# First softmax of a graph layer: its flags made in the gather's stage, its leaky function on ScalarE and TensorE, its loop rows shared out over two stages

## The reference

```
e = jnp.einsum('ehd,hd->eh', src, a_src) + jnp.einsum('ehd,hd->eh', dst, a_dst)
e = e + edge_bias
e = jnp.where(e > 0, e, ALPHA * e)                                  # ALPHA = 0.2
max_per_node = jax.ops.segment_max(e, col, num_segments=num_nodes)
exp_scores = jnp.exp(e - max_per_node[col])
sum_per_node = jax.ops.segment_sum(exp_scores, col, num_segments=num_nodes)
attn = exp_scores / jnp.maximum(sum_per_node[col], 1e-12)
msg = src * edge_gate * attn[..., None]
```

## Time and profile before

| what | value |
|---|---|
| profiled execution, its own time | 8693.18 us |
| its span, first to last instruction | 8691.1 us |
| mean granted TensorE clock (1.0 is 2.4 GHz) | 0.772 |
| busy: TensorE, VectorE, ScalarE, GpSimd | 5916.9, 6071.0, 1746.5, 6425.4 us |
| `stage_gate` | 52.5 to 2115.9 us |
| `stage_softmax` | 2115.9 to 2288.0 us |
| `stage_aggregate` | 2288.0 to 2858.2 us |
| `stage_first_update` | 2858.2 to 2968.5 us |
| `stage_move` | 2968.5 to 5130.6 us |

### The profile page before, as it was taken

One profiled execution on the slowest core, in us unless ns is written; L12 is line 12 of the kernel. 1 busy time (PEld: TensorE's weight loads), 2 busy tenths in 40 slices (PEclk: granted clock), 3 DMA queues, 4 the chain that ended last, 5 costly groups with the idle time before them and its releaser, 6 DMA issues. The chain is left out here.

```text
span 8691.1 us, 192168 instructions
## 1 busy us (share of the span) xinstructions
PE 5916.9 (68%) x40472; PEld 4854.3 (56%) x40473; DVE 6071.0 (70%) x12108; ACT 1746.5 (20%) x5063; POOL 6425.4 (74%) x7809
## 2 busy tenths in 40 slices
PE   6666666665788587777777549999588830566442
PEld 4455555553677466666666437777378720455332
DVE  5555555556777887777777448888599899898335
ACT  1111111111211444444444102222500010111000
POOL 6777777776788377777777778887277778877774
PEclk6555555555899799999999669999799965899555
DMA  6778888875477266666666669998189953798664
GB/s 198 218 216 219 219 217 220 218 219 168 130 210 211 70 212 205 207 206 206 207 206 207 211 196 268 273 270 239 35 245 263 260 145 87 197 255 237 163 163 110
DMA packets 1900193, 1739.84 MB, mean 200 GB/s; under 512 B 163065, under 2 KB 1624495, under 8 KB 1899807
## 3 DMA queue, kind: packets, MB, share of 16 engines
q1 hardware_dynamic: 1216980, 816.75, 32.2%
q10 hardware_dynamic: 496812, 471.17, 19.3%
q0 software_dynamic: 186160, 449.72, 18.5%
HBM read 1285.39 MB, written 452.43 MB: 200 GB/s over the span
## 5 line engine op out<-in xcount | busy, mean ns | idle before, releaser
L1877 POOL DMA_INDIRECT z_xg<-table,srci x1664 | 1781.6, 1071 | 512.7 <-issue 457.4
L1414 POOL DMA_INDIRECT sorted<-e_score,srci x1612 | 1628.2, 1010 | 602.8 <-issue 427.2
L461 POOL DMA_INDIRECT g_xg<-table,srci x1612 | 1553.9, 964 | 539.5 <-issue 470.0
L481 PE MATMUL g_psg<-g_wg,g_eT 128*128 128x136 f32 x3224 | 1027.5, 474 | 0.0
L1957 PE MATMUL z_ps<-z_wrow,z_oh 128*128 128x132 f32 x3712 | 652.1, 330 | 501.9 <-issue 332.6
L1735 PE MATMUL n_ps<-n_row,n_oh 128*128 128x257 f32 x3712 | 881.2, 389 | 93.2 <-DVE n_row L1711 79.3
L1957 PEld LDWEIGHTS z_ps<-z_wrow,z_oh 128*128 128x128 f32 x3712 | 559.4, 228 | 594.6 <-issue 557.3
L481 PEld LDWEIGHTS g_psg<-g_wg,g_eT 128*128 128x128 f32 x3224 | 769.3, 324 | 191.9 <-issue 191.9
L1735 PEld LDWEIGHTS n_ps<-n_row,n_oh 128*128 128x128 f32 x3712 | 677.7, 190 | 298.0 <-issue 216.4
L479 PE MATMUL g_psg<-g_bias,g_ones 3*128 3x272 bf16 x806 | 318.4, 395 | 675.6 <-DVE g_es L570 646.8
L1473 PE MATMUL m_psx<-acc,e_score 128*128 x3608 | 600.5, 317 | 197.8 <-DVE e_score L1598 122.9
(11 more groups left out here) (426 smaller groups left out, 12696.0 us busy)
## 6 DMA issues: line engine op xcount, KB each, us to landing
n_row<-sorted SPq DMA_DIRECT2D x464, 520.0 KB, 4.4
z_buf<-gathered ACTq DMA_DIRECT2D x464, 256.0 KB
g_keys<-dst_row ACTq DMA_DIRECT2D x451, 256.0 KB, 3.8
ag_buf<-gated SPq DMA_DIRECT2D x451, 256.0 KB, 3.3
m_keys<-dst_row ACTq DMA_DIRECT2D x451, 256.0 KB
gathered<-z_xg SPq DMA_DIRECT2D x416, 256.0 KB
gated<-g_y SPq DMA_DIRECT2D x403, 256.0 KB
g_eT<-in_attr_t SPq DMA_DIRECT2D x402, 256.0 KB
```

The lines of the kernel that those rows point to most:

```text
L461: nc.gpsimd.indirect_dma_start(out=xg[:, u, j, :], out_offset=None, in_=v.table[:, :], in_offset=bass.IndirectOffsetOnAxis(ap=v.srci[:, t: ...
L481: last = nc.tensor.matmul(psg[u % 2][:, h, j * W:(j + 1) * W], eT[:, u % R, (h * H + j) * P:(h * H + j + 1) * P], wg[:, :], start=False, s ...
L1414: nc.gpsimd.indirect_dma_start(out=v.sorted[:, :], out_offset=bass.IndirectOffsetOnAxis(ap=place[:, t:t + 1], axis=0), in_=rows[:, u, j, : ...
L1877: nc.gpsimd.indirect_dma_start(out=xg[:, u, j, :], out_offset=None, in_=v.table[:, :], in_offset=bass.IndirectOffsetOnAxis(ap=v.dsti[:, t: ...
```

## The change

It has five parts.

1. The flags are made in `stage_gate`, by the same eight VectorE instructions, in bf16 in place of f32, from a window of destinations that SP loads into the space of `y`. They stand ahead of the stage's first one-hots.
2. The leaky function leaves VectorE. ScalarE makes `bent`, the absolute value of 0.4 times the head's scores, one instruction for each head. `turn_in` then makes 0.6 times the score plus `bent` with two ordinary matmuls a block (against `steep`, which is 0.6 times the identity, and against the identity) in place of one transpose.
3. Loop rows go in groups of four. Five groups (20 rows) stay in `stage_softmax`. The other 29 are scattered at the end of GpSimd's list in `stage_first_update`, with two buffer sets.
4. The four writes to `firsts` are issued by SP with the loads of the groups 4 to 7 of `stage_gate`.
5. `stage_move` takes `lo` and `hi` over from `stage_gate`. GpSimd fills `rows` with ones, ScalarE copies the keys into `facts`, and ScalarE no longer waits for `s_split`.

```diff
@@ stage_gate
+                sp.dma_start(win[:, 0:TR], window).then_inc(s_win, 16)
...
                 def load(g, u, use):
                     if later(g, R):
                         sp.wait_ge(s_gpe, g - R + 1)
+                    if isinstance(g, int) and R <= g < R + 4:
+                        sp.wait_ge(s_none, 1)
+                        sp.dma_start(empty[:, (g - R) * TR:(g - R + 1) * TR], none[:, :]).then_inc(s_empty, 16)
...
-                sp.wait_ge(s_none, 1)
-                for n in range(4):
-                    sp.dma_start(empty[:, n * TR:(n + 1) * TR], none[:, :]).then_inc(s_empty, 16)
...
+                flagged = chain(dve, s_fl)
+                dve.wait_ge(s_win, 48)
+                for d, (r, g) in enumerate(((fl.rf, fl.gf), (fl.rb, fl.gb))):
+                    way = slice(None, None, -1) if d else slice(None)
+                    edge = TR - 1 if d else 0
+                    flagged(nc.vector.tensor_tensor(r[:, :], win[:, 1:TR + 1], win[:, 2 * d:2 * d + TR], ALU.not_equal))
+                    flagged(nc.vector.tensor_scalar(r[:, :], r[:, :], -BIG, None, ALU.mult))
+                    flagged(nc.vector.tensor_tensor_scan(g[:, way], r[:, way], r[:, way], 0.0, ALU.min, ALU.min))
+                    flagged(nc.vector.memset(r[:, edge:edge + 1], -BIG))
+                dve.wait_ge(s_fl, 8)
@@ new, called by stage_softmax (first=0, last=5, one set) and stage_first_update (5 to 13, two sets)
+def loop_rows(nc, v, pool, loops, s_lp, done, s_loop, first, last):
+    sets, LR = len(s_loop), LOOP_ROWS
+    for n, q in enumerate(range(first, last)):
+        at = n % sets
+        if n >= sets:
+            pool.wait_ge(s_loop[at], 16 * LR * (n // sets))
+        some = min(LR, NB - q * LR)
+        nc.gpsimd.tensor_scalar(loops[:, at, 0:some, TAKING + 1], v.blk[:, q * LR:q * LR + some], v.part[:, 0:1], None,
+                                ALU.add).then_inc(s_lp, 1)
+        pool.wait_ge(s_lp, done + n + 1)
+        for i in range(some):
+            b = q * LR + i
+            nc.gpsimd.indirect_dma_start(
+                out=v.sorted[:, :], out_offset=bass.IndirectOffsetOnAxis(ap=v.loop_at[:, b:b + 1], axis=0),
+                in_=loops[:, at, i, :], in_offset=None).then_inc(s_loop[at], 16)
...
@@ stage_softmax
                         for k in range(a, z):
-                            last = nc.tensor.transpose(ps_in[m % 2][:, (k - a) * P:(k - a + 1) * P], e[:, k::KR, h],
-                                                       v.ident[:, :])
+                            to = ps_in[m % 2][:, (k - a) * P:(k - a + 1) * P]
+                            nc.tensor.matmul(to, e[:, k::KR, h], steep[:, :], start=True, stop=False)
+                            last = nc.tensor.matmul(to, bent[:, k::KR], v.ident[:, :], start=False, stop=True)
...
+                def bend(h):
+                    if h:
+                        act.wait_ge(s_tin, h * len(parts))
+                    nc.scalar.activation(bent[:, :], e[:, :, h], ACT.Abs, scale=0.4).then_inc(s_leaky, 1)
+
+                bend(0)
                 take(0)
+                bend(1)
                 for t in range(H + 3):
                     if 0 <= t - 3 < H:
                         give(t - 3)
                     if t + 1 < H:
                         take(t + 1)
+                    if t + 2 < H:
+                        bend(t + 2)
...
-                    if t + 2 < H:
-                        leaky(t + 2)
@@ stage_first_update, GpSimd
+                nc.gpsimd.memset(loops[:, :, :, :], 0.0).then_inc(s_lp, 1)
...
+                loop_rows(nc, v, pool, loops, s_lp, 2, s_loop, LOOPS_FIRST, -(-NB // LOOP_ROWS))
@@ stage_move
+                nc.gpsimd.memset(rows[:, :, :, :], 1.0).then_inc(s_set, 1)
...
-                    else:
-                        act.wait_ge(s_split, 5)
...
+                for n, key in ((2, v.srck), (3, v.dstk)):
+                    nc.scalar.activation(facts[:, :, n], key, ACT.Copy).then_inc(s_facts, 1)
+                act.wait_ge(s_facts, 2)
+                act.wait_ge(s_set, 1)
...
-                nc.vector.memset(rows[:, :, :, :], 1.0).then_inc(s_set, 1)
...
-                link(nc.vector.tensor_scalar(lo_i, v.srci[:, :], P - 1, None, ALU.bitwise_and))
```

More of the change, by code:

```diff
@@ L612, in _, with stage_softmax @@
                 nc.vector.tensor_copy(hist[:, :], psc[:, 0:NBX]).then_inc(s_end, 1)
-def stage_softmax(nc, v, e, hist, run, below):
-    H, SETS, LR = X8, 4, 5
+def loop_rows(nc, v, pool, loops, s_lp, done, s_loop, first, last):
[13 more added lines that the diff above has]
+                in_=loops[:, at, i, :], in_offset=None).then_inc(s_loop[at], 16)
+    for at in range(sets):
+        rows = sum(min(LR, NB - q * LR) for n, q in enumerate(range(first, last)) if n % sets == at)
+        pool.wait_ge(s_loop[at], 16 * rows)
+LOOP_ROWS, LOOPS_FIRST = 4, 5
+def stage_softmax(nc, v, e, hist, run, below, fl):
+    H, SETS = X8, 4
     sem = v.sem
-    s_b, s_bpe, s_win, s_fl, s_whole = (sem("b_" + n) for n in ("dve", "pe", "win", "fl", "whole"))
-    s_lp, s_pad, s_loop = sem("l_lp"), sem("l_pad"), v.pool_dma_sem("l_loop")
+    s_b, s_bpe, s_fl, s_whole = (sem("b_" + n) for n in ("dve", "pe", "fl", "whole"))
+    s_lp, s_pad, s_loop = sem("l_lp"), sem("l_pad"), [v.pool_dma_sem("l_loop")]
     s_neg, s_tin, s_v, s_vb = sem("f_neg"), sem("f_tin"), sem("f_v"), sem("f_vb")
@@ L797, in _ @@
                 flagged = chain(dve, s_fl)
[L798 to L805 removed]
+                nc.vector.tensor_copy(edges[:, 0:1], gf[:, TR - 1:TR])
+                flagged(nc.vector.tensor_copy(edges[:, 1:2], gb[:, 0:1]))
                 nc.vector.memset(carry[:, :, 0, 0:1], -BIG)
@@ L1184, in stage_first_update @@
     s_x, s_tr, s_xt, s_h, s_row = (sem("u_" + n) for n in ("x", "tr", "xt", "h", "row"))
+    s_lp, s_loop = sem("u_lp"), [v.pool_dma_sem(f"u_loop{n}") for n in range(2)]
     with ExitStack() as mem:
@@ L1337, in _, with stage_move @@
                         rows(i - 5)
-def stage_move(nc, v, held, run, steps, follows, below, sorted_steps, spare):
+def stage_move(nc, v, held, run, steps, follows, below, sorted_steps, spare, split):
     sem = v.sem
     R, U, S = 4, 4, SLOTS
-    s_split, s_set, s_fix = sem("m_split"), sem("m_set"), sem("m_fix")
+    s_split, s_set, s_fix, s_facts = sem("m_split"), sem("m_set"), sem("m_fix"), sem("m_facts")
     s_oh, s_cnt, s_run, s_ohtb = (sem("r_" + n) for n in ("oh", "cnt", "run", "ohtb"))
@@ L1544, in _ @@
                 nc.vector.memset(ohhi[:, :, :, 1, :], 0.0).then_inc(s_fix, 1)
-                for n, key in ((2, v.srck), (3, v.dstk)):
-                    nc.vector.tensor_copy(facts[:, :, n], key)
                 def onehots(g, u, use):
@@ L2567, in build @@
             e_score = sb("e_score", [P, TR, X8], F32, layer)
-            stage_gate(nc, v, e_score, gated, hist, steps_e)
-            recycle(nc, v)
-            stage_softmax(nc, v, e_score, hist, run, below)
+            split = [sb("src_" + k, [P, TR], BF16, layer) for k in ("lo", "hi")]
+            with ExitStack() as until:
+                fl = Env()
+                fl.rf, fl.rb, fl.gf, fl.gb = (sb("node_" + k, [P, TR], BF16, until) for k in ("rf", "rb", "gf", "gb"))
+                stage_gate(nc, v, e_score, gated, hist, steps_e, fl, split)
+                recycle(nc, v)
+                stage_softmax(nc, v, e_score, hist, run, below, fl)
             acc = sb("acc0", [P, NBX, W], F32, layer)
@@ L2575, in build @@
             recycle(nc, v)
-            stage_move(nc, v, held, run, steps_e, follows, below, steps_s, flat(e_score[:, :, :]))
+            stage_move(nc, v, held, run, steps_e, follows, below, steps_s, flat(e_score[:, :, :]),
+                       split)
         both.close()
```

86 lines of the change are left out of this document (30 added, 56 removed).

## The result

The changed kernel took 8710.01 us (median of 8 runs, 8703.09 to 8713.82) where the kernel before took 8678.96 (8 runs, 8674.83 to 8685.21): 1.0031 times as long, 95% interval 1.0022 to 1.004. The forecast was 8633 us, faster by 46 us. It became slower by 31 us. The two profiled executions differ by 21 us (spans of 8691.1 and 8712.1 us); the one of before lies 14 us above the median of its runs, the one of after 4 us, and the traces can only explain those 21 us.

The account below looks back on a forecast made before the run. GpSimd was taken to bound gather and move, VectorE the softmax's steady turns, ScalarE the first update. Terms 8 - 7.7 - 36 + 0 - 11 = -46.7 us gave 8633 us, likeliest range 8620 to 8648.

Parts of the forecast that it names:

- The step that failed: Softmax, TensorE: the new `turn_in` priced as 52 passes, 11.2 us cold or 5.6 warm, 7.7 when beginning cold.
- Rival A: Softmax: TensorE's clock stays at 1.2 GHz, softmax about 205 us instead of 172, net +22, 8702 us; chance 0.04.
- A second step: Softmax steady turns: ScalarE adds one `bend` to 5.42 us of its turn and stays far below the bound.
- Gate, head: Gate's start: flags added on VectorE delay GpSimd's gathers; 8 us longer, bounds 0 and 10.
- the row of 4.03 us: Softmax before: a scatter issued beside the flags' scan took 4.03 us, a plain one 0.97; basis for 8 us in the gate.
- Gate, tail: Gate's end: without SP's four late writes the next stage starts earlier; -7.7 us, bounds -5.5 and -8.
- Move: Move's set-up: fill on GpSimd and copies on ScalarE bring the first scatter earlier; -11 us, bounds -14 and -4.
- End of the softmax: Softmax ends with ScalarE's last exponential instead of a DMA; next stage 0.5 us later, at softmax start + 135.5.
- rival B: First update: loop rows, at 3.2 us a row, outlast the update; +21 us, 8654 us; chance 0.10.
- Update: First update: GpSimd's fill and 29 loop rows stay hidden, landing at most to 2946, before ScalarE ends at 2964.3; 0 us.
- The tail of 34.9 us behind `forward(7)`: Softmax: from `forward(7)` to the last exponential's end, without leaky or `turn_in`, so 34.9 us was to stay.
- Rival C: Softmax: VectorE binds, not TensorE, 11.9 us a turn, and `turn_in(0)` warm; about -9 more, 8624 us; chance 0.05.

## Why the prediction was wrong

**The step that failed** is in the softmax, "A `turn_in` of 26 matmuls is 52 passes like those of `turn_out`: 0.215 us a pass at a clock of 0.50 and 0.107 at 0.98". All 52 passes were priced by contiguous loads. The passes aren't alike. `turn_out` takes its stationary operand from 128 neighbouring elements; `turn_in` takes it with steps of 416 bytes (`e[:, k::KR, h]`) and 52 bytes (`bent[:, k::KR]`). Removing one step took that matmul from 0.51 to 0.22 us with nothing else changed on TensorE; removing the other took it from 0.64 to 0.22, where only the other operand changed too, from `steep` to the identity, both contiguous. So 15.0 us stand where the forecast put 5.6 to 11.2. The transposes of before have the 416-byte step and show next to nothing of it: 13 in 3.08 us, 0.24 each, where a contiguous pass took 0.215 at the same clock. The only stepped rows that the forecast had the earlier trace rows thus pointed the wrong way. Why a transpose, one pass of 0.13 us, escapes what an ordinary pass of 0.32 us pays stays open. The bounds were drawn from the clock; none came from the operand's layout.

The Trainium skill, page "SBUF — State Buffer", section "Door 1: The DMA port swizzle", says in a note that SBUF is read in lines of 16 bytes and that each access that crosses to a new line pays. Both steps cross a line at every element. The traces agree in direction for ordinary matmuls (0.32 and 0.26 us a pass against 0.11), though the two steps differ, and not for transposes (0.13). That note was the rule to weigh against this change, and the prediction did not weigh it.

**Rival A** gave a softmax of 205 us and slower by 22, nearly what came, with a chance of 0.04. That it came so near is luck. Its reason was wrong: the pair takes 1.15 us at either level, and at 1.00 throughout the matmuls with the 416-byte step are as slow. Nor did ordinary matmuls keep the clock high, the ground on which the prediction would have let this rival fall: it was 0.72 over the softmax, about that of before (0.71). The low clock adds something in `turn_out`: behind a stepped `turn_in` the clock stood at 0.50, and with `bent` contiguous, where it stayed at 1.00, a turn lost 5.4 us (23.9 to 18.5) of which 13 x 0.29 = 3.8 are `turn_in`.

**A second step is in doubt**, hidden by the first: "ScalarE adds one `bend` to 5.42 us of its turn and stays far below." By share it does (8.93 of 23.92). With two such instructions and contiguous operands TensorE waited for ScalarE's order. How much one `bend` would cost beside a fast `turn_in` was not tried alone.

**Right, with its size.** Gate, head: the last gather ended at 2098.2 us before and at 2103.3 after, +5.1 us, forecast 8; over the experiments it ended at 2094.8 to 2098.2 in three kernels without the flags there and at 2101.0 to 2103.5 in six with them. The means are 6.4 us apart, single pairs 3 to 9. VectorE's flags and the gathers beside them:

```profile
79.89 0.59 DVE L565 TENSOR_SCALAR node_rf<-node_rf 128x1664 bf16<-128x1664 bf16 x1
80.51 3.62 DVE L566 TENSOR_TENSOR_SCAN node_gf<-node_rf 128x1664 bf16<-128x1664 bf16 x1
```

```profile
77.30 3.37 POOL L468 DMA_INDIRECT g_xg<-table,srci  x1 [0.30 <-issue]
80.97 3.92 POOL L468 DMA_INDIRECT g_xg<-table,srci  x1 [0.30 <-issue]
85.19 1.82 POOL L468 DMA_INDIRECT g_xg<-table,srci  x1 [0.30 <-issue]
87.32 3.92 POOL L468 DMA_INDIRECT g_xg<-table,srci  x1 [0.30 <-issue]
```

A gather of 0.94 us takes 3.92 beside a scan of 3.62, so the row of 4.03 us was the right one to go by. What the prediction set against it, from the Trainium skill, page "SBUF — State Buffer", section "Who interferes with whom", does not hold for this scan, whose two inputs are the same tile. Gate, tail: 17.7 to 9.5 us, -8.2, forecast -7.7. Move: -10.8, forecast -11, by a path that was only in part the forecast's. GpSimd's fill held VectorE for 7.04 us, which the forecast did not have, so ScalarE's first copy of turned sources came 10.5 us into the stage instead of 7.5 to 9.5. End of the softmax: 0.27 us to the next stage, and no loop row is the last of a stage; rival B did not occur. Update: +2.0 instead of 0. VectorE's first instruction there takes 2.02 us, where it was 0.37, beside GpSimd's fill of the loop rows:

```profile
2891.49 2.02 DVE L1246 TENSOR_SCALAR u_inv<-acc 128x400 f32<-128x400 f32 x1 [0.33 <-PEq L1021]
```

The forecast had hidden that fill behind GpSimd's own wait and had not asked whom it stops. The tail of 34.9 us behind `forward(7)` held (34.7), and `forward(0)` came at S + 21.1 instead of 13, 7.3 us of it again `turn_in` and 0.7 the `bend`, 3.23 us instead of 2.5. Rival C's sum has a slip: its terms give -11 rather than -9, which moves nothing.

## What to carry to other kernels

Price a matmul by a row whose stationary operand has the same step and the same form (ordinary or transpose), not by one of the same shape; where an ordinary f32 matmul would load with a step, let the engine that writes the tile write it block by block. Before calling an engine "far below" the bound, look for what its new instruction stands between in its own list. And when a part moves the bound to another engine, check whether the other parts' gains still lie on the path: beside heads that end at S + 208 the loop rows' 31 us were worth nothing, and the flags' move cost the gate its 5 to 6 us and gave the softmax nothing.

## What the runs showed of the hardware

- An ordinary 128 x 128 f32 matmul took 0.22 us with a contiguous stationary operand at the high clock, 0.51 with a step of 52 bytes and 0.64 with 416 bytes, the last two at either level of the clock. A transpose with 416 bytes took 0.13 at the high level and 0.24 at the low one.
- TensorE's clock fell from 0.97 to 0.50 within a `turn_in` in which it was busy for all 14.5 us; with half of those operands contiguous the granted clock was 1.00 through two whole turns, in which it was busy for 18.0 of 18.5 us.
- A fill on GpSimd stopped VectorE, as a fill on VectorE stopped GpSimd (a gather of 10.27 us beside one of 11.15). A copy of 50 elements took 7.04 us beside GpSimd's fill of 7.03, and 0.19 us with the fill behind it:

```profile
3003.82 7.04 DVE L1561 COPY m_cnt<-run 128x50 f32<-128x50 f32 x1 [8.44 <-PEq L2512]
```

```profile
2927.59 0.19 DVE L1561 COPY m_cnt<-run 128x50 f32<-128x50 f32 x1 [8.65 <-PEq L2512]
```
